# The last 64 inner rows of the experts as one K=128 product; routing constants made in the attention block; final norm in the tiles' block

## The chip, the cores and the metric

The kernel runs on one core of a Trainium2 chip. The metric is the device time of one execution in microseconds (us); three executions of the kernel before are given, and one more was profiled.

## What is computed

Two post-norm layers on x of shape (8, 512, 256), all in float32: 4,096 tokens of width 256.

```python
x = layernorm(x + attention_with_biases(x))            # 16 heads of 16, full
h = x + causal_attention(rmsnorm(x, g1))               # 16 heads of 16, with rope
y = h + moe(rmsnorm(h, g2))                            # 8 experts, top 2, inner size 704
out = layernorm(x + y)

def moe(xf):                                           # weights wg, wu (256 x 704), wd (704 x 256) per expert
    probs = softmax(xf @ w_router); topw, topi = top_k(probs, 2)
    g = silu(xf @ wg[e]); u = xf @ wu[e]
    return sum over the two experts of topw_normalised * ((g * u) @ wd[e])
```

## The kernel before, in words

Float32 products are made on TensorE (PE) as sums of float16 products: a value is split into a high part and a low part (what the rounding to float16 left), and a product is high x high + high x low + low x high, accumulated in one PSUM region.

The program is a row of stages. `attention_layers` (both attentions, the split of the experts' weights into parts, the router's logits) is one block of five engine programs; `route_tokens` (which tokens go to which expert, VectorE (DVE) mostly) is the next; `expert_tiles` follows, then `combine` (sum of the residual and the final layer norm). Each stage ends in two steps: the block's own end, at which every engine drains and meets the others (L271 for the attention, L1279 for the routing, L1484 for the tiles, L1734 for the final stage; the numbers are the lines that the profile gives), and `stage_semaphores`, which clears the stage's semaphores and has all engines meet again (L55, L56). Work of the next stage starts only after that.

**Routing.** GpSimd (POOL) writes eleven small constants (`iota`, `memset`, one `affine_select`; L1329 to L1345), counted by the semaphore `made`. DVE first clears rows 64 to 127 of the last chunk of `w_down` (L1397), then waits for `made` to reach 11 and for its own clearing, and then runs a chain of some 60 operations, each waiting for the one before. SyncE (SP) loads the weights of expert 0 meanwhile, then those of experts 1 to 3 (`load_experts`, L1263 to L1270), each expert waiting for the loads of the one before.

**Tiles.** Rows sorted by expert are worked on in 39 tiles of 256 rows. In tile after tile PE turns the gathered x (8 transposes, L1591), makes gate and up products in three groups (66 matmuls with 256 columns, L1606) and the down product of the tile before (36 matmuls, L1628), the latter between group 0 and group 1 of the following tile. The inner size 704 is 5 chunks of 128 rows and a sixth of 64 (`FT` = 6, `FR` = 64). The down product reads h (high part, low part) as the stationary operand and `w_down` as the moving one, once for each half of 128 rows:

```python
for half in range(2):
    for f in range(FT):
        for hh, wh in ((0, 0), (0, 1), (1, 0)):
            mm = pe.matmul(ps_y[:, s, half], h[:, s, hh, f, ...], w_down[:, e, wh, f, :])
```

So the sixth chunk takes three matmuls of a half like the others, with rows 64 to 127 of both operands zero. ScalarE (ACT) makes silu and the high part of h (L1669 to L1680), DVE the product gate x up (L1709) and the low part (L1715); the sixth chunk's are instructions on 64 partitions. DVE also scales the result by the token's share (L1697). POOL issues, on its own queue, the gathers of x (L1538) and of the shares (L1564) and the scatter that adds y into `h` in DRAM (L1552, two for a tile); a scatter waits until that of the tile before has landed. After the last tile POOL waits for the last two tiles' scatters and ends its program.

**Final stage** (`combine`). SP loads the eight sequences (512 KB each, L1750) from `h`; DVE takes mean and variance (L1776, L1779), POOL makes scale and shift in four small operations (L1764 to L1769), ACT applies them (32 activations, L1787), SP stores (L1753). POOL writes three constants first (L1759).

Of the kernel before, what the change touches and what calls it, by code (L numbers as in the profile page):

```python
# [214 lines left out]
def attention_layers(nc, t, xT_dram, x_dram, x1_dram, matrices):  # L215
# [55 lines left out]
    with ExitStack() as ctx:  # L271
# [57 lines left out]
        w_hi, w_lo, rest_filled = sem("w_hi"), sem("w_lo"), sem("rest_filled")  # L329
        block = ctx.enter_context(nc.Block())  # L330
# [181 lines left out]
        def _(pool):  # L512
# [109 lines left out]
            for n in range(FIRST, LAST):  # L622
                u, g = n // G, n % G
                if n % 2 == 0:
                    h = (n + 6) // 2
                    if plain(h // 2):
                        split_high(h)
                        split_low(h)
                    if g == 0:
                        factors(u - 2)  # L630
                        split_x(u + 2)
                    else:
                        part_low(u - 2)
                    turn_half(h)
                else:
                    h = (n + 5) // 2
                    if causal(h // 2):
                        split_high(h)
                        split_low(h)
                    if g == 1:  # L640
                        bias(u - 1)
                    normalise((n - 3) // 2)
                    if g == 3:
                        add_residual(u - 1)
                for m in weights_at(n):
                    split_weights(m)

# [606 lines left out]
def load_experts(sync, t, experts):  # L1254


    for e in experts:
# [6 lines left out]
        if e > 0:  # L1264
            sync.wait_ge(t.down_loaded, 64 * e)
        for hl in range(2):
# [3 lines left out]
            sync.dma_start(t.w_down[0:FR, e, hl, FT - 1], down[(FT - 1) * P:F]).then_inc(t.down_loaded, 16)  # L1270


def route_tokens(nc, t):
# [5 lines left out]
    with ExitStack() as ctx:  # L1279
# [3 lines left out]
        rank = sb("rank", [P, NT, E], F32)  # L1283
# [7 lines left out]
        earlier, ones = sb("earlier", [P, P], F32), sb("ones", [P, P], F32)  # L1291
        totals = sb("totals", [P, E, NT], F32)
        keep = sb("keep", [P, E, NT], F32)
# [7 lines left out]
        own = sb("own", [P, HI], F32)  # L1301
        tile_start = sb("tile_start", [P, MT, 1], F32)
# [3 lines left out]
        count_hi, count_lo = sb("count_hi", [P, 1, HI], BF16), sb("count_lo", [P, 1, P], BF16)  # L1306
# [4 lines left out]
        tile_no, row_no = sb("tile_no", [P, 2 * NT, 1], BF16), sb("row_no", [P, 1], F32)  # L1311
# [4 lines left out]
        made, did, exp_done, totalled, hot_done, by_row_done, inverse_mm, turned = map(sem, (  # L1316
            "made", "did", "exp_done", "totalled", "hot_done", "by_row_done", "inverse_mm", "turned"))
# [9 lines left out]
        @block.gpsimd  # L1327
        def _(pool):
            iota = lambda out, pattern, base, mult: pool.iota(  # L1329
                out, pattern, base=base, channel_multiplier=mult,  # L1330
                allow_small_or_imprecise_dtypes=True).then_inc(made, 1)
            iota(rank[:], [[0, NT], [-1, E]], E, 0)
            iota(tile_start[:], [[SLOT, MT]], 0, 0)
            iota(count_hi[:], [[1, HI]], 0, 0)
            iota(count_lo[:], [[1, P]], 0, 0)
            iota(tile_no[:], [[1, 2 * NT]], 1, 0)
            iota(row_no[:], [[0, 1]], 0, 1)
            iota(own[:].rearrange("p (m h) -> p m h", h=REST // P), [[0, MT], [P, REST // P]], P - T - REST, 1)
            pool.memset(ones[:], 1.0).then_inc(made, 1)
            pool.memset(keep[:], 1.0).then_inc(made, 1)  # L1340
            pool.wait_ge(made, 9)

            pool.affine_select(out=earlier[:], in_=ones[:], pattern=[[1, P]], compare_op=ALU.is_gt, fill=0.0,
                               base=0, channel_multiplier=-1).then_inc(made, 1)
            pool.memset(keep[:, :, 0:1], 0.0).then_inc(made, 1)  # L1345
            pool.wait_ge(made, 11)

        MADE = 11
# [19 lines left out]
        def _(pe):  # L1368
            pe.wait_ge(made, MADE)
# [17 lines left out]
        def _(vector):  # L1387
# [89 lines left out]
def expert_tiles(nc, t):  # L1477
# [6 lines left out]
    with ExitStack() as ctx:  # L1484
# [16 lines left out]
        cleared, h_cleared = sem("indices_cleared"), sem("h_cleared")  # L1501
# [4 lines left out]
        gu_mm, gate_out, h_out, h_hi, h_lo = map(pair, ("gu_mm", "gate_out", "h_out", "h_hi", "h_lo"))  # L1506
        block = ctx.enter_context(nc.Block())
# [6 lines left out]
        def _(sync):  # L1514
# [5 lines left out]
            sync.wait_ge(t.down_loaded, 64 * E)  # L1520

        @block.gpsimd
        def _(pool):

            pool.memset(take[:], 0).then_inc(cleared, 1)
# [54 lines left out]
            for s in range(2):  # L1580
                pool.wait_ge(stored[s], 32 * (LAST + 2 - s))

        @block.tensor
        def _(pe):
# [30 lines left out]
            def down(r, s):  # L1615
                e = expert_of(r, s)
                pe.wait_ge(t.down_loaded, e * 64 + 64)
                pe.wait_ge(y_out[s], r)
                for half in range(2):
                    c = 0  # L1620
                    for f in range(FT):
# [4 lines left out]
                        for hh, wh in ((0, 0), (0, 1), (1, 0)):  # L1626
# [3 lines left out]
                                           start=c == 0, stop=c == 3 * FT - 1)  # L1630
# [16 lines left out]
            pe.wait_ge(h_cleared, 1)  # L1647
# [10 lines left out]
        def _(act):  # L1658
# [29 lines left out]
            tile(LAST + 1, 0, None)  # L1688

        @block.vector  # L1690
        def _(vector):
# [8 lines left out]
            def tile(r, s, before):  # L1700
                for i in range(FG):
# [20 lines left out]
            vector.memset(h[FR:P, :, :, FT - 1], 0.0).then_inc(h_cleared, 1)  # L1722
# [7 lines left out]


def combine(nc, t, out):

    with ExitStack() as ctx:  # L1734
        sem = ctx.enter_context(stage_semaphores(nc, "c_"))
        sb = lambda n, s, d: ctx.enter_context(nc.sbuf_tensor("c_" + n, s, d))
        z, res = sb("z", [P, B, QT, D], F32), sb("res", [P, B, QT, D], F32)
        stats, mean_var = sb("stats", [P, B, QT, 6], F32), sb("mean_var", [P, B, QT, 2], F32)
        small = sb("small", [P, B, 4, QT], F32)
        constants = sb("constants", [P, 3, QT], F32)  # L1740
        loaded = [sem(f"loaded{b}") for b in range(B)]
        stored, stat_out, aggregated, power, mid_out, rstd_out, shift_out, done = map(sem, (
            "stored", "stat_out", "aggregated", "power", "mid_out", "rstd_out", "shift_out", "done"))
        block = ctx.enter_context(nc.Block())
        rows = lambda x, b: x[b * S:(b + 1) * S].rearrange("(p q) n -> p q n", q=QT)

        @block.sync
        def _(sync):
            for b in range(B):
                sync.dma_start(z[:, b], rows(t.h_dram[REST:], b)).then_inc(loaded[b], 16)  # L1750
            for b in range(B):
                sync.wait_ge(done, QT * (b + 1))
                sync.dma_start(rows(out, b), res[:, b]).then_inc(stored, 16)  # L1753
            sync.wait_ge(stored, 16 * B)

        @block.gpsimd
        def _(pool):
            for i, value in enumerate((-0.5, LN_EPS, -1.0)):
                pool.memset(constants[:, i], value).then_inc(power, 1)  # L1759
            pool.wait_ge(power, 3)  # L1760
            for b in range(B):
                pool.wait_ge(aggregated, QT * (b + 1))  # L1762
                mean, var = mean_var[:, b, :, 0], mean_var[:, b, :, 1]
                pool.tensor_tensor(small[:, b, 0], var, constants[:, 1], ALU.add).then_inc(mid_out, 1)  # L1764
                pool.tensor_tensor(small[:, b, 2], mean, constants[:, 2], ALU.mult).then_inc(mid_out, 1)  # L1765
                pool.wait_ge(mid_out, 2 * b + 2)
                pool.tensor_tensor(small[:, b, 1], small[:, b, 0], constants[:, 0], ALU.pow).then_inc(rstd_out, 1)  # L1767
                pool.wait_ge(rstd_out, b + 1)
                pool.tensor_tensor(small[:, b, 3], small[:, b, 2], small[:, b, 1], ALU.mult).then_inc(shift_out, 1)  # L1769

        @block.vector
        def _(vector):
            for b in range(B):
                vector.wait_ge(loaded[b], 16)
# [5 lines left out]

        @block.scalar
        def _(act):
            for b in range(B):
                act.wait_ge(rstd_out, b + 1)
                act.wait_ge(shift_out, b + 1)  # L1785
                for q in range(QT):
                    act.activation(res[:, b, q], z[:, b, q], ACT.Identity, bias=small[:, b, 3, q:q + 1],  # L1787
                                   scale=small[:, b, 1, q:q + 1]).then_inc(done, 1)


def feed_forward_kernel(nc, a, out):

    with ExitStack() as top:
# [13 lines left out]
        t.tile_expert = sb("tile_expert", [P, MT], I32)  # L1807
        with ExitStack() as ctx:
# [14 lines left out]
        with ExitStack() as ctx:  # L1823
# [9 lines left out]
            expert_tiles(nc, t)  # L1833
            combine(nc, t, out)
# [33 lines left out]
```

## Time and profile before

| | |
|---|---|
| time, median of 3 runs | 1481.46 us (1475.09, 1481.46, 1482.32) |
| the profiled execution | 1479.55 us |
| its span in the trace | 1477.6 us |
| PE busy | 1279.7 us, 87% of the span |
| DVE / ACT / POOL busy | 949.5 / 829.9 / 801.2 us |
| attention stage | up to about 913 us |
| routing | 915 to 957 us |
| expert tiles | 958 to 1444 us |
| final stage | 1450 to 1477.6 us |

Busy times of engines overlap. The span runs from the first to the last instruction; the profiled execution's own time is 1.95 us longer than its span. A stage's time is set by the engine or chain that ends it, which the timelines of its end show.

### The profile page before, as it was taken

How to read it: one execution, taken by the hardware profiler on the slowest of the kernel's cores; microseconds unless marked ns; L12 is line 12 of the kernel's file. 1: busy time of each engine (PE TensorE's matmuls, PEld its weight loads, DVE VectorE, ACT ScalarE, POOL GpSimd, SP SyncE). 2: the span in 40 equal slices, each digit the busy share in tenths (PEclk: the TensorE clock that was granted, in tenths of full speed). 3: DMA queues.
4: the chain of work that ended last, by engine and by line, in shares of the span. 5: the costliest groups of instructions: out<-in, count | busy, mean ns of one | idle time of the engine just before them, and what ended most of it. 6: DMA issues, size and time to landing. Idle time of an engine off the chain costs nothing. (4 is left out here: it accounts for less than half of the span.)

```text
span 1477.6 us, 33278 instructions
## 1 busy us (share of the span) xinstructions
PE 1279.7 (87%) x11533; PEld 712.1 (48%) x11534; DVE 949.5 (64%) x1766; ACT 829.9 (56%) x1672; POOL 801.2 (54%) x834
## 2 busy tenths in 40 slices
PE   1699999999999999999999963389999999999980
PEld 0222222232323444444444432378888888888870
DVE  6378888888898887977888613834444444444433
ACT  4148787888888776666676741133444344333334
POOL 2322565475546566765564333056666666666643
PEclk9769999999999999999999975589999999999995
DMA  4416767676767878887775534693222222222326
GB/s 127 86 36 171 179 180 200 188 197 201 196 178 216 216 224 210 234 217 207 166 190 156 132 95 129 178 261 61 43 43 44 45 46 43 43 43 44 42 29 235
DMA packets 158365, 204.21 MB, mean 138 GB/s; under 512 B 31088, under 2 KB 120688, under 8 KB 158256
## 3 DMA queue, kind: packets, MB, share of 16 engines
q1 hardware_dynamic: 140784, 182.29, 45.3%
q0 software_dynamic: 17472, 20.50, 8.9%
q8 instruction: 64, 1.05, 0.3%
q14 instruction: 45, 0.37, 0.1%
HBM read 111.20 MB, written 82.87 MB: 131 GB/s over the span
## 5 line engine op out<-in xcount | busy, mean ns | idle before, releaser
L987 ACT ACTIVATE a_probs<-a_ps_s 128x512 f32<-128x512 f32 (+2 forms) x896 | 460.0, 569 | 159.4 <-PE a_ps_s L782 154.3
L1056 DVE TENSOR_REDUCE a_shift_max<-a_ps_m 128x1 f16<-128x512 f32 x512 | 320.4, 682 | 70.5 <-PE a_ps_m L787 69.1
L787 PE MATMUL a_ps_m<-a_qkx 48*128 48x128 f16 (+3 forms) x1408 | 284.3, 301 | 21.1 <-DMA a_qkx<-a_qk_dram 8.9
L1606 PE MATMUL e_ps_gu<-e_xT,w_up 128*128 128x256 f16 x2574 | 297.8, 273 | 2.6 <-ACT e_xT L1661 2.4
L782 PE MATMUL a_ps_s<-a_qkx 49*128 49x128 f16 (+3 forms) x1408 | 275.4, 295 | 15.3 <-ACT a_probs L987 15.3
L1606 PEld LDWEIGHTS e_ps_gu<-e_xT,w_up 128*128 x2574 | 249.3, 98 | 36.1 <-issue 7.1
L883 PE MATMUL a_ps_o<-a_probs,a_v_one 128*32 128x512 f32 (+3 forms) x2048 | 234.1, 530 | 2.8 <-ACT a_o L994 2.7
L782 PEld LDWEIGHTS a_ps_s<-a_qkx 49*128 49x128 f16 x1408 | 89.6, 94 | 266.9 <-ACT a_probs L987 155.8
L1552 POOL DMA_INDIRECT h<-e_y,e_put x78 | 124.8, 1600 | 90.2 <-DVE e_y L1697 60.2
L1628 PE MATMUL e_ps_y<-w_down,e_h 128*128 x1404 | 162.7, 273 | 7.6 <-issue 5.0
L552 POOL TENSOR_TENSOR a_o_half<-a_o_half,a_inv_half 128x512 f32<-128x512 f32 x32 | 40.6, 1270 | 227.4 <-DMA a_inv_half<-a_inv_dram 227.4
L1709 DVE TENSOR_TENSOR e_h<-e_gate,e_ps_gu 128x512 f32<-128x512 f32 (+2 forms) x156 | 82.6, 550 | 126.2 <-ACT e_gate L1669 87.3
L1669 ACT ACTIVATE e_gate<-e_ps_gu 128x512 f32<-128x512 f32 x78 | 46.6, 597 | 200.9 <-PE e_ps_gu L1606 128.8
L1628 PEld LDWEIGHTS e_ps_y<-w_down,e_h 128*128 128x128 f16 x1404 | 127.9, 97 | 40.1 <-issue 14.9
L1056 DVE TENSOR_REDUCE a_neg_off<-a_ps_m 128x1 f32<-128x384 f32 (+2 forms) x256 | 138.1, 543 | 8.9 <-PE a_ps_m L787 8.1
L1715 DVE TENSOR_TENSOR e_h<-e_h 128x512 f16<-128x512 f32 (+2 forms) x156 | 83.5, 556 | 89.1 <-ACT e_h L1673 46.2
L539 POOL CAST a_qk<-a_q 128x1024 f16<-128x1024 f32 x32 | 33.2, 1036 | 157.6 <-DVE a_q L1111 96.0
L670 PE MATMUL a_ps_x<-a_xT,w_proj 128*128 128x512 f16 x384 | 101.6, 404 | 18.3 <-POOL a_xT L520 15.8
L787 PEld LDWEIGHTS a_ps_m<-a_qkx 48*128 48x128 f16 x1408 | 84.1, 94 | 63.9 <-DVE a_shift_max L1056 36.7
L1056 DVE TENSOR_REDUCE a_neg_max<-a_ps_m 128x4 f32<-128x512 f32 x128 | 87.7, 685 | 41.0 <-PE a_ps_m L787 40.2
L1564 POOL DMA_INDIRECT e_share<-weights,e_find x78 | 81.2, 1041 | 42.2 <-issue 42.2
L1538 POOL DMA_INDIRECT e_x<-part,e_take x78 | 81.2, 1041 | 41.5 <-issue 40.3
(195 smaller groups left out, 1661.0 us busy)
## 6 DMA issues: line engine op xcount, KB each, us to landing
a_qkx<-a_qk_dram SPq DMA_DIRECT2D x192, 128.0 KB, 4.5
a_qk_dram<-a_qk SPq DMA_DIRECT2D x32, 512.0 KB, 5.4
a_o_dram<-a_o SPq DMA_DIRECT2D x64, 256.0 KB, 2.7
a_o_half<-a_o_dram SPq DMA_DIRECT2D x32, 256.0 KB
a_inv_half<-a_inv_dram SPq DMA_DIRECT2D x32, 256.0 KB
part<-a_part SPq DMA_DIRECT2D x16, 512.0 KB, 5.8
a_q_swap<-a_q SPq DMA_DIRECT2D x64, 128.0 KB, 3.9
a_w_in<-in_wg SPq DMA_DIRECT2D x16, 352.0 KB, 5.4
```

What stands on the lines that cost most here:

```text
L670: mm = pe.matmul(ps_x[:], t.w_proj[:, 4 * layer + w, wh, k, m * P:(m + 1) * P], xT[:, u % 2, xh, k, :], start=n == 0, stop=n == 5)
L782: return pe.matmul(out, kx[first:first + 49, r, pair, kt * P:(kt + 1) * P], qx[first:first + 49, r, pair, q0:q1], start=start, stop=stop)
L787: return pe.matmul(out, qx[first:first + 48, r, pair, q * P:(q + 1) * P], kx[first:first + 48, r, pair, k0:k1], start=start, stop=stop)
L883: mm = pe.matmul(ps_o[32 * j:32 * (j + 1), S - w:S], v_one[:, u % 2, kt, g * HG + j, :], probs[:, kt // 2, j, first:first + w], start=kt = ...
L987: act.activation(dst, src, ACT.Exp).then_inc(exp_out, 1)
L1056: vector.tensor_reduce(out, src, AX.X, ALU.max, negate=True).then_inc(max_out, 1)
L1538: pool.indirect_dma_start(x[:, s, half], None, t.part_dram, bass.IndirectOffsetOnAxis(ap=take[:, s, half:half + 1], axis=0)).then_inc(gath ...
L1552: pool.indirect_dma_start(t.h_dram, bass.IndirectOffsetOnAxis(ap=put[:, s, half:half + 1], axis=0), y[:, s, half], None, compute_op=ALU.ad ...
L1606: mm = pe.matmul(ps_gu[:, bank, kind, f % 2], w[:, ds(e, 1)].rearrange("p o f -> p (o f)"), xT[:, s, xh, k, :], start=n == 0, stop=n == 5)
L1628: mm = pe.matmul(ps_y[:, s, half], h[:, s, hh, f, half * P:(half + 1) * P], w[:, ds(e, 1)].rearrange("p o f -> p (o f)"), start=c == 0, st ...
L1709: op = vector.tensor_tensor(h32[0:rows, bank, m], gate[0:rows, bank, m], ps_gu[0:rows, bank, 1, m], ALU.mult)
L1715: op = vector.tensor_tensor(h[0:rows, s, 1, f], h32[0:rows, bank, m], h[0:rows, s, 0, f], ALU.subtract)
```

## The change

Three parts.

1. The low part of h's sixth chunk (64 rows) is written into rows 64 to 127 of the high part's chunk, and rows 64 to 127 of the high `w_down` chunk hold a second copy of the same 64 weight rows. One matmul then makes high x high + low x high, a second one (with the low weights, whose rows 64 to 127 stay zero) high x low. The down product takes 34 matmuls for a tile instead of 36. Each expert's load has one more transfer (64 x 256 float16); only the low half of `w_down` is cleared, by POOL in the routing stage, and h is not cleared at all.
2. The eleven constants of the routing are written by POOL at the end of its attention program; they live in tensors of the whole kernel. The routing's DVE and PE programs no longer wait for them.
3. `combine` is gone; its instructions stand at the end of the engines' programs in the tiles' block, with the loaded sums and the results in the space of `w_up`. SP itself waits for the last scatters and then loads. POOL writes the three constants at the start of the tiles' block.

```diff
@@ attention_layers, POOL, after the loop @@
+            iota = lambda out, pattern, base, mult: pool.iota(
+                out, pattern, base=base, channel_multiplier=mult,
+                allow_small_or_imprecise_dtypes=True).then_inc(made, 1)
+            iota(t.rank[:], [[0, NT], [-1, E]], E, 0)
...
+            pool.memset(t.keep[:, :, 0:1], 0.0).then_inc(made, 1)
+            pool.wait_ge(made, 11)
@@ load_experts @@
-            sync.wait_ge(t.down_loaded, 64 * e)
+            sync.wait_ge(t.down_loaded, 80 * e)
...
-            sync.dma_start(t.w_down[0:FR, e, hl, FT - 1], down[(FT - 1) * P:F]).then_inc(t.down_loaded, 16)
+            for first in ((0, FR) if hl == 0 else (0,)):
+                sync.dma_start(t.w_down[first:first + FR, e, hl, FT - 1],
+                               down[(FT - 1) * P:F]).then_inc(t.down_loaded, 16)
@@ route_tokens @@
         def _(pool):
-            iota = lambda out, pattern, base, mult: pool.iota(
...
-            pool.wait_ge(made, 11)
+            pool.memset(t.w_down[FR:P, :, 1, FT - 1], 0.0).then_inc(padded_out, 1)
+            pool.wait_ge(padded_out, 1)
...
-            pe.wait_ge(made, MADE)
             pe.wait_ge(ready_both, 1)
...
-            vector.memset(t.w_down[FR:P, :, :, FT - 1].rearrange("p e h n -> p (e h) n"), 0.0).then_inc(padded_out, 1)
-            vector.wait_ge(made, MADE)
-            vector.wait_ge(padded_out, 1)
             source = t.logits
@@ expert_tiles @@
+        zr = w_up[:].rearrange("p e h k f -> p (e h k f)")[:, 0:4 * B * QT * D].bitcast(F32).rearrange(
+            "p (z b q n) -> p z b q n", z=2, b=B, q=QT)
+        z, res = zr[:, 0], zr[:, 1]
...
+            for s in range(2):
+                sync.wait_ge(stored[s], 32 * (LAST + 2 - s))
+            for b in range(B):
+                sync.dma_start(z[:, b], rows(t.h_dram[REST:], b)).then_inc(sum_loaded[b], 16)
...
         def _(pool):
+            for i, value in enumerate((-0.5, LN_EPS, -1.0)):
+                pool.memset(constants[:, i], value).then_inc(power, 1)
...
-                        for hh, wh in ((0, 0), (0, 1), (1, 0)):
+                        for hh, wh in ((0, 0), (0, 1)) if f == FT - 1 else ((0, 0), (0, 1), (1, 0)):
...
-                                           start=c == 0, stop=c == 3 * FT - 1)
+                                           start=c == 0, stop=c == 3 * FT - 2)
...
-            pe.wait_ge(h_cleared, 1)
             turn(0, 0)
...
-                        op = vector.tensor_tensor(h[0:rows, s, 1, f], h32[0:rows, bank, m], h[0:rows, s, 0, f],
-                                                  ALU.subtract)
+                        low = h[0:P, s, 1, f] if rows == P else h[FR:2 * FR, s, 0, f]
+                        op = vector.tensor_tensor(low, h32[0:rows, bank, m], h[0:rows, s, 0, f], ALU.subtract)
...
-            vector.memset(h[FR:P, :, :, FT - 1], 0.0).then_inc(h_cleared, 1)
             tile(0, 0, None)
```

The order of instructions moves at two places. The first is POOL at the end of the attention stage and in the routing (`L55 ISA` is the semaphore clearing between two stages, a branch the end of a block's program). Before:

```order
L608 TENSOR_TENSOR a_part<-a_hid,a_part 128x4x256
L271 UNCONDITIONAL_BRANCH
L55 ISA
L1327 UNCONDITIONAL_BRANCH
L1329 IOTA r_rank 128x256
L1329 IOTA r_tile_start 128x39
L1329 IOTA r_count_hi 128x78
```

And in the change (`a_part` is now L609; it and the first four `IOTA` stand right ahead of this piece):

```order
L649 IOTA tile_no 128x64
L649 IOTA row_no 128x1
L649 IOTA own 128x78
L659 MEMSET ones 128x128
L660 MEMSET keep 128x256
L662 AFFINE_SELECT earlier<-ones 128x128
L664 MEMSET keep 128x8
L271 UNCONDITIONAL_BRANCH
L55 ISA
L1343 UNCONDITIONAL_BRANCH
L1345 MEMSET w_down 64x8x256
```

All eleven constants now stand ahead of the block's end; between the block's end and the tiles POOL has the clearing of `w_down` alone.

The second is SP at the end of the tiles. `L1484` is the end of the tiles' block. Before:

```order
L1268 DMA w_down<-w_down_lo 128x5x256
L1270 DMA w_down<-w_down_lo 64x256
L1484 UNCONDITIONAL_BRANCH
L1747 UNCONDITIONAL_BRANCH
L1750 DMA c_z<-h 128x1024 x8
L1753 DMA out<-c_res 128x1024 x8
L1734 UNCONDITIONAL_BRANCH
```

And in the change:

```order
L1287 DMA w_down<-w_down_lo 128x5x256
L1290 DMA w_down<-w_down_lo 64x256
L1530 DMA w_up<-h 128x1024 x8
L1533 DMA out<-w_up 128x1024 x8
L1478 UNCONDITIONAL_BRANCH
```

The loads of the sums follow the weight loads in the same program, with no end of a block between.

## Rows read from the trace of the kernel before

**Rows 1.** Busy time by stretch, whole core: stretch, PE, PEld, DVE, ACT, POOL, clock, DMA, GB/s

```profile
960.00:1000.00 40.00, 33.70 (x300) 28.36 (x301) 12.30 (x23) 15.07 (x25) 22.87 (x29) 0.89 0.93 258
1100.00:1400.00 300.00, 296.21 (x2757) 253.81 (x2756) 128.71 (x251) 118.84 (x225) 198.35 (x226) 1.00 0.28 44
```

**Rows 2.** Timeline of PE, 963 to 1000 us: start, duration, instruction, idle before

```profile
979.37 4.16 PE L1628 MATMUL e_ps_y<-w_down,e_h 128*128 x36 [0.39 <-issue]
983.36 2.78 PE L1606 MATMUL e_ps_gu<-e_xT,w_up 128*128 128x256 f16 x24
...
995.23 2.78 PE L1606 MATMUL e_ps_gu<-e_xT,w_up 128*128 128x256 f16 x24
```

**Rows 3.** What PE waited for, 960 to 1440 us: us in total, times, longest

```profile
PE e_ps_xT L1591 <- DMA e_x<-part,e_take: 8.5, 1, 8.5
PE e_ps_y L1628 <- issue: 5.0, 16, 0.4
PE e_ps_y L1628 <- DVE e_h L1715: 2.6, 4, 1.6
PE e_ps_gu L1606 <- ACT e_xT L1661: 2.4, 2, 1.4
```

**Rows 4.** Timeline, 905 to 965 us, all engines

```profile
907.81 2.12 POOL L608 TENSOR_TENSOR a_part<-a_hid,a_part 128x1024 f16<-128x1024 f32 x1 [2.87 <-ACT a_part L1030]
...
912.79 0.19 DVE L1130 COPY logits<-a_ps_x 128x32 f32<-128x32 f32 x1 [0.97 <-PE a_ps_x L733]
...
914.73 0.59 POOL L1329 IOTA r_rank<- 128x256 f32 x1 [4.80 <-POOLq L56]
...
915.21 1.76 DVE L1397 MEMSET w_down<- 64x2048 uint32 x1 [2.23 <-PEq L56]
...
917.45 0.42 DVE L1402 TENSOR_REDUCE r_best<-logits 128x32 f32<-128x256 f32 x1 [0.48 <-POOL r_keep L1345]
```

**Rows 5.** Instructions of line 271, the attention block's end: duration ns, start us

```profile
L271 SPq COMPARE_BRANCH  x1: 33/33/33, 913.4 to 913.4; - x1
```

**Rows 6.** Instructions of line 1279, the routing block's end

```profile
L1279 SPq DRAIN  x1: 370/370/370, 944.1 to 944.1; - x1
L1279 DVEq DRAIN  x1: 10/10/10, 957.0 to 957.0; - x1
```

**Rows 7.** Timeline, 1435 to 1477.6 us

```profile
1440.96 1.55 POOL L1552 DMA_INDIRECT h<-e_y,e_put  x1 [0.30 <-issue]
1449.83 4.78 SPq L1750 DMA_DIRECT2D c_z<-h  x8
1449.83 0.17 POOL L1759 MEMSET c_constants<- 128x4 f32 x3 [7.32 <-POOLq L56]
...
1455.96 0.20 POOL L1764 TENSOR_TENSOR c_small<-c_mean_var,c_constants 128x4 f32<-128x4 f32 x1 [5.95 <-DVE c_mean_var L1779]
```

**Rows 8.** Instructions of line 1484, the tiles block's end

```profile
L1484 POOLq COMPARE_BRANCH  x1: 41/41/41, 1444.6 to 1444.6; - x1
L1484 POOLq DRAIN  x1: 4221/4221/4221, 1444.8 to 1444.8; - x1
```

**Rows 9.** Timeline, 1200 to 1225 us

```profile
1201.78 1.62 POOL L1552 DMA_INDIRECT h<-e_y,e_put  x1 [2.40 <-DVE e_y L1697]
...
1206.95 0.75 DVE L1715 TENSOR_TENSOR e_h<-e_h 128x256 f16<-128x256 f32 x2 [0.79 <-ACT e_h L1680]
...
1207.14 4.19 PE L1628 MATMUL e_ps_y<-w_down,e_h 128*128 x36
...
1213.11 1.62 POOL L1552 DMA_INDIRECT h<-e_y,e_put  x1 [0.86 <-POOL e_put L1546]
```

**Rows 10.** Groups by line and shape, 960 to 1440 us: ACT, then DVE

```profile
L1675 ACT ACTIVATE e_gate<-e_ps_gu 128x256 f32<-128x256 f32 x39 | 14.9, 383 | 13.6 <-PE e_ps_gu L1606 13.4 <-issue 0.2
L1676 ACT ACTIVATE e_gate<-e_ps_gu 64x256 f32<-64x256 f32 x39 | 14.8, 380 | 0.5
L1715 DVE TENSOR_TENSOR e_h<-e_h 64x256 f16<-64x256 f32 x39 | 16.0, 410 | 0.0
```

More of the change, by code:

```diff
@@ L1310, in route_tokens @@
         by_row = sb("by_row", [P, 2 * NT, HI], BF16)
-        tile_no, row_no = sb("tile_no", [P, 2 * NT, 1], BF16), sb("row_no", [P, 1], F32)
+        rank, tile_start, keep, earlier, ones = t.rank, t.tile_start, t.keep, t.earlier, t.ones
+        own, count_hi, count_lo, tile_no, row_no = t.own, t.count_hi, t.count_lo, t.tile_no, t.row_no
         inverse = sb("inverse", [P, P], F32)
@@ L1506, in expert_tiles @@
         gu_mm, gate_out, h_out, h_hi, h_lo = map(pair, ("gu_mm", "gate_out", "h_out", "h_hi", "h_lo"))
+        zr = w_up[:].rearrange("p e h k f -> p (e h k f)")[:, 0:4 * B * QT * D].bitcast(F32).rearrange(
+            "p (z b q n) -> p z b q n", z=2, b=B, q=QT)
+        z, res = zr[:, 0], zr[:, 1]
+        stats, mean_var = sb("stats", [P, B, QT, 6], F32), sb("mean_var", [P, B, QT, 2], F32)
+        small = sb("small", [P, B, 4, QT], F32)
+        constants = sb("constants", [P, 3, QT], F32)
+        sum_loaded = [sem(f"sum_loaded{b}") for b in range(B)]
+        out_stored, stat_out, aggregated, power, mid_out, rstd_out, shift_out, done = map(sem, (
+            "out_stored", "stat_out", "aggregated", "power", "mid_out", "rstd_out", "shift_out", "done"))
+        rows = lambda x, b: x[b * S:(b + 1) * S].rearrange("(p q) n -> p q n", q=QT)
         block = ctx.enter_context(nc.Block())
@@ L1519, in _ @@
                 sync.wait_ge(t.up_loaded[hl], 48 * E)
-            sync.wait_ge(t.down_loaded, 64 * E)
+            sync.wait_ge(t.down_loaded, 80 * E)
+            for s in range(2):
+                sync.wait_ge(stored[s], 32 * (LAST + 2 - s))
+            for b in range(B):
+                sync.dma_start(z[:, b], rows(t.h_dram[REST:], b)).then_inc(sum_loaded[b], 16)
+            for b in range(B):
+                sync.wait_ge(done, QT * (b + 1))
+                sync.dma_start(rows(out, b), res[:, b]).then_inc(out_stored, 16)
+            sync.wait_ge(out_stored, 16 * B)
         @block.gpsimd
         def _(pool):
+            for i, value in enumerate((-0.5, LN_EPS, -1.0)):
+                pool.memset(constants[:, i], value).then_inc(power, 1)
             pool.memset(take[:], 0).then_inc(cleared, 1)
@@ L1581, in _ @@
                 pool.wait_ge(stored[s], 32 * (LAST + 2 - s))
+            pool.wait_ge(power, 3)
+            for b in range(B):
+                pool.wait_ge(aggregated, QT * (b + 1))
+                mean, var = mean_var[:, b, :, 0], mean_var[:, b, :, 1]
+                pool.tensor_tensor(small[:, b, 0], var, constants[:, 1], ALU.add).then_inc(mid_out, 1)
+                pool.tensor_tensor(small[:, b, 2], mean, constants[:, 2], ALU.mult).then_inc(mid_out, 1)
+                pool.wait_ge(mid_out, 2 * b + 2)
+                pool.tensor_tensor(small[:, b, 1], small[:, b, 0], constants[:, 0], ALU.pow).then_inc(rstd_out, 1)
+                pool.wait_ge(rstd_out, b + 1)
+                pool.tensor_tensor(small[:, b, 3], small[:, b, 2], small[:, b, 1], ALU.mult).then_inc(shift_out, 1)
         @block.tensor
@@ L1688, in _ @@
             tile(LAST + 1, 0, None)
+            for b in range(B):
+                act.wait_ge(rstd_out, b + 1)
+                act.wait_ge(shift_out, b + 1)
+                for q in range(QT):
+                    act.activation(res[:, b, q], z[:, b, q], ACT.Identity, bias=small[:, b, 3, q:q + 1],
+                                   scale=small[:, b, 1, q:q + 1]).then_inc(done, 1)
         @block.vector
@@ L1729, in _ @@
             empty_y(LAST + 1, 0)
[L1732 to L1748, printed above, removed]
-            for b in range(B):
[L1750 to L1774, printed above, removed]
@@ L1779, in _ @@
                     vector.bn_aggr(mean_var[:, b, q], stats[:, b, q]).then_inc(aggregated, 1)
[L1781 to L1788, printed above, removed]
 def feed_forward_kernel(nc, a, out):
@@ L1807, in feed_forward_kernel @@
         t.tile_expert = sb("tile_expert", [P, MT], I32)
+        t.rank, t.tile_start = sb("rank", [P, NT, E], F32), sb("tile_start", [P, MT, 1], F32)
+        t.keep, t.earlier, t.ones = sb("keep", [P, E, NT], F32), sb("earlier", [P, P], F32), sb("ones", [P, P], F32)
+        t.own = sb("own", [P, HI], F32)
+        t.count_hi, t.count_lo = sb("count_hi", [P, 1, HI], BF16), sb("count_lo", [P, 1, P], BF16)
+        t.tile_no, t.row_no = sb("tile_no", [P, 2 * NT, 1], BF16), sb("row_no", [P, 1], F32)
         with ExitStack() as ctx:
```

48 lines of the change are left out of this document (19 added, 29 removed).

## The prediction

> **What bounds the kernel now.** I read four views in turn: busy time by stretch, what PE waits for among the tiles, the timelines of the two stage borders that the change touches, and the instructions at the ends of the blocks. The reader should see three different limits. Among the tiles PE is busy 296.21 of 300 us at the full granted clock [rows 1], and all its waits from 960 to 1440 us sum to 18.5 us, 8.5 of them one wait for the first gather [rows 3]: a matmul removed there is worth its own time. In the routing PE has nothing to do and one chain of DVE operations sets the end; it starts at 917.45 us, when POOL's last constant is there [rows 4]. In the final stage loads, DVE, POOL and ACT follow one another, and everything hangs on when the first load is issued, 1449.83 us [rows 7].
>
> **Part 1, the down product.** It removes 2 matmuls of 36 in each of 39 tiles, 78 in all. The price of one comes from start to start, since ends overlap: 36 matmuls fill 979.37 to 983.36 us, 111 ns each [rows 2]; over 300 us the mean is 296.21/2757 = 107 ns, narrower transposes included [rows 1]. I take 111: 78 x 0.111 = 8.7 us (8.4 at the least). All of it is on the path unless another engine has to be waited for, and two could be.
>
> DVE: the low part of the sixth chunk must be there when PE gets to chunk 4, where it waits for both last chunks. In the tile at 1207 us the pair of low operations ends at 1206.95 + 0.75 = 1207.70, and PE, which begins at 1207.14, is 12 matmuls or 1.33 us further at 1208.47 [rows 9]: 0.77 us of slack, and nothing ahead of chunk 4 changes. The operation itself, on 64 partitions (0.410 us) [rows 10], now writes to other partitions than it reads. No row shows DVE doing that; the nearest is ACT, which reads rows 64 to 127 and writes rows 0 to 63 in 380 ns, beside 383 ns for the same width unshifted [rows 10]. So zero; the price of its being otherwise is the last rival.
>
> POOL: from one scatter to the next it needs 1213.11 - 1201.78 = 11.3 us in a tile in which its own copy, not y, was what it waited for last [rows 9]. PE's tile takes 995.23 - 983.36 = 11.87 us [rows 2] and would take 11.65. That is 0.3 us of room, thin but enough.
>
> The extra weight transfers (one for each expert, 32 KB) go to SP's queue. For experts 0 to 3 SP is done at 944.1 us while DVE comes to the block's end at 957.0 [rows 6]; four more transfers at the 4.78/8 = 0.6 us that SP takes to issue one [rows 7] are far below 12.9. Experts 4 to 7 are loaded while the first tiles run, with the DMA engines 93% busy [rows 1], and PE did not wait for them [rows 3]. Zero, at worst 1 us where they meet the gathers. The clearing of h is hidden behind the first gather's 8.5 us [rows 3]: zero.
>
> **Part 2, the constants.** DVE's first useful operation starts at 917.45 us; without its own clearing of 1.76 us and the wait for POOL it starts where the clearing did, 915.21 [rows 4]. Gain 2.24 us, and the chain behind it moves as a whole. The constants take POOL 917.45 - 914.73 = 2.7 us at most [rows 4]. At the end of the attention POOL is free from 907.81 + 2.12 = 909.93 us [rows 4], so it would be done by 912.7, while DVE's last copy ends at 912.98 and SP comes to the block's end at 913.4 [rows 4, 5]. They are covered with 0.7 us to spare; without the cover they would cost at most their 2.7 us. The clearing of half of `w_down` on POOL has the whole DVE chain as cover. On the other side POOL now writes three more constants ahead of the first gather: 0.17 us [rows 7], exposed, since PE waits for that gather.
>
> **Part 3, the final norm.** POOL sees the last scatters landed at 1444.6 us and goes to the block's end. There its drain takes 4.221 us [rows 8], then come the meeting, the clearing and the second meeting, and SP issues the first load at 1449.83 [rows 7]. In the change SP waits for the same semaphores itself and can issue at about 1444.7: a gain of 5.1 us. What the drain waits for is not shown. POOL's last scatter instruction ended at 1442.51 [rows 7], so it is nothing that I can name. If POOL really is occupied until 1449.0 us, the norm does not suffer: its first small operation stands at 1455.96 now [rows 7] and would be due at 1455.96 - 5.1 = 1450.9. Everything behind the first load moves as it is. The Trainium skill (VectorE: DVE Perf Modes, The DRAIN you can't avoid) says that the drains around a program, on all five engines, are about 12 ns constant, beside a longer one that belongs to DVE's operations. By that rule a drain on POOL is worth nothing by itself, and the 4.2 us would be something else that stays; the row says 4.221 us, and the sum goes by the row.
>
> **Sum.** 8.7 + 2.24 + 5.1 - 0.17 = 15.9 us less. The profiled execution took 1479.55 us, so the changed kernel should take 1463.7, rounded to 1464. The median of the three runs is 1.9 us above the profiled one and the lowest 4.5 below it, so the sum may be off by that alone.
>
> **Rivals.** *The time behind the drain stays.* What occupied POOL for 4.2 us could hold the loads or POOL's small operations as well, past the point worked out above. Then only the rest of the border is saved, 5.2 - 4.2 = 1.0 us, and the time is 1463.7 + 4.1 = 1468. For it: the cause of the drain is unknown. Against: POOL already knows at 1444.6 that the data have landed. *The tile's length is not PE's.* If POOL's chain of 11.3 us with its scatters, or a wait that PE's model hides, sets the 11.87, 78 matmuls give nothing: 1463.7 + 8.7 = 1472.4. For it: the 0.3 us of room; against: PE's few waits [rows 3] and its 99% of busy time [rows 1]. *The constants are not covered.* POOL may be slower at them beside the attention's last work; past 0.7 us of slack up to 2 us come back, 1466. *Slower: PE waits for the shifted low part.* If DVE's write to other partitions takes 0.41 + t, PE waits t - 0.77 in every tile. The gains are used up at t = 0.77 + 15.9/39 = 1.18 us, that is an operation of 1.6 us, four times its present length; from 1.37 us on the kernel is slower by over 0.5%. At five times (t = 1.64) it is 34 us of waiting, 1498. For it: no DVE row with a shift. Against: ACT's pair of rows, where the shift costs nothing [rows 10].
>
> **Chances.** The forecast as it stands 0.66, the drain's time staying 0.13, no gain in the tiles 0.10, constants exposed 0.06, slower 0.05. The spread of the runs before gives the forecast's own range, 1459 to 1467; adding the case of the drain and that of the constants reaches 1471. What is left out are the two ends, together a little under 0.2 with the noise. A measurement of this kernel can tell some 0.5% (7.4 us) from no change. Faster by more than that: 0.66 + 0.13 + 0.06 and a small part of the 1472 case, 0.87; within it 0.08; slower 0.05.
>
> **What would show it.** Down matmuls 1326 instead of 1404; a tile of 11.65 us; DVE's first reduce of the routing right after the stage border, 2.2 us earlier against the end of the attention; the first load of the sums within 0.3 us of the last scatters' landing, and POOL's long drain, if it is still there, beside ACT's work. I am wrong if PE shows waits for L1715's successor or for gathers in most tiles, if POOL's constants end after SP's arrival at the attention's end, or if the first small operation of POOL in the final norm starts later than 2 us after the first load has landed.

## The result and the profile after

The changed kernel takes 1460.6 us (median of 4 runs, 1459.44 to 1469.85) against 1478.28 us before (4 runs, 1474.09 to 1482.32): a ratio of the means of 0.9892 (a fifth run of the change, 1461.24 us, is in it), 95% interval 0.9847 to 0.9938, or 16 us less; the medians lie 17.7 us apart. The forecast was 15.9 us less, 1464 us, with a range of 1459 to 1471.

The profiled execution of the changed kernel is the longest of its four, 1469.85 us with a span of 1468.1. Its attention stage, which the change hardly touches, ended 7.3 us later than in the profile of before: the last copy of the logits starts at 920.06 us instead of 912.79. Over all thirteen traces of this study that moment lies between 907.5 and 920.1 us, with and without the constants, so whole spans say little here and stages say much. What follows compares lengths inside the two traces. From the start of that copy to the end of the span it is 1477.6 - 912.79 = 564.8 us before and 1468.1 - 920.06 = 548.0 after: 16.8 us less.

Busy time by stretch of the changed kernel (columns as in rows 1):

```profile
1100.00:1400.00 300.00, 295.84 (x2757) 254.29 (x2755) 134.22 (x258) 120.45 (x229) 199.30 (x231) 1.00 0.28 45
```

PE is as busy as before and does as many matmuls in 300 us, 2757 [rows 1]; a tile merely needs 108 of them instead of 110. Its timeline, to be held against rows 2:

```profile
1195.88 3.93 PE L1654 MATMUL e_ps_y<-w_down,e_h 128*128 x34 [0.30 <-issue]
1199.64 2.78 PE L1632 MATMUL e_ps_gu<-e_xT,w_up 128*128 128x256 f16 x24
...
1207.35 3.97 PE L1654 MATMUL e_ps_y<-w_down,e_h 128*128 x34
1211.16 2.78 PE L1632 MATMUL e_ps_gu<-e_xT,w_up 128*128 128x256 f16 x24
```

Here 34 matmuls fill 3.76 us, still 111 ns each, and this tile takes 11.52 us. Tiles come in two lengths that take turns: from the start of the third down product to that of the 35th the mean of a tile is 11.99 us before (mostly 11.7 and 12.3) and 11.75 after (mostly 11.4 and 12.1). What PE waited for, 960 to 1437 us (rows 3):

```profile
PE e_ps_xT L1617 <- DMA e_x<-part,e_take: 8.5, 1, 8.5
PE e_ps_y L1654 <- issue: 5.4, 17, 0.4
PE e_ps_y L1654 <- DVE e_h L1747: 2.3, 3, 1.6
PE e_ps_gu L1632 <- ACT e_xT L1686: 1.4, 1, 1.4
```

No wait took the place of the removed work. Timeline of the border from attention to routing (rows 4):

```profile
915.09 2.12 POOL L609 TENSOR_TENSOR a_part<-a_hid,a_part 128x1024 f16<-128x1024 f32 x1 [2.87 <-ACT a_part L1049]
...
917.16 0.59 POOL L649 IOTA rank<- 128x256 f32 x1
...
919.74 0.11 POOL L664 MEMSET keep<- 128x8 f32 x1
920.06 0.19 DVE L1149 COPY logits<-a_ps_x 128x32 f32<-128x32 f32 x1 [0.96 <-PE a_ps_x L752]
922.00 1.80 POOL L1345 MEMSET w_down<- 64x2048 f16 x1 [2.15 <-POOLq L56]
...
922.04 0.42 DVE L1396 TENSOR_REDUCE r_best<-logits 128x32 f32<-128x256 f32 x1 [1.79 <-PEq L56]
```

and who came to the block's end when (rows 5):

```profile
L271 POOLq DRAIN  x1: 34/34/34, 920.0 to 920.0; - x1
L271 DVEq DRAIN  x1: 223/223/223, 920.1 to 920.1; - x1
L271 SPq COMPARE_BRANCH  x1: 38/38/38, 920.7 to 920.7; - x1
```

The constants fill the gap between POOL's last work and SP's arrival. They end at 919.85 us, some 0.85 us ahead of it, and with POOL's drain some 0.6 us. The final stage (rows 7) and the end of the tiles' block (rows 8):

```profile
1436.66 1.55 POOL L1568 DMA_INDIRECT h<-e_y,e_put  x1 [0.30 <-issue]
1440.55 3.74 SPq L1530 DMA_DIRECT2D w_up<-h  x8
...
1446.26 0.20 POOL L1602 TENSOR_TENSOR e_small<-e_mean_var,e_constants 128x4 f32<-128x4 f32 x1 [8.04 <-DVE e_mean_var L1766]
```

```profile
L1478 POOLq DRAIN  x1: 4487/4487/4487, 1459.6 to 1459.6; - x1
L1478 ACTq DRAIN  x1: 3972/3972/3972, 1460.0 to 1460.0; - x1
L1478 SPq COMPARE_BRANCH  x1: 33/33/33, 1466.5 to 1466.5; - x1
```

The first load follows the start of the last scatter instruction by 3.89 us, 8.87 before [rows 7]. POOL's drain has not gone. It is 4.487 us long, more than 20 us after the last scatter, and lies beside ACT's last work and the stores, where it costs nothing. POOL's first small operation comes 2.00 us after DVE's first of the final norm, 1.98 before.

### The profile page after: what moved, and what is told of

Its sections match the earlier page's. It is cut to its first block and busy times, and to the rows that moved or that the text cites. A ratio compares the mean times of both kernels' runs of the same rounds, so it can differ in the third digit from the quotient of the medians.

```text
span 1468.1 us, 33103 instructions
## 1 busy us (share of the span) xinstructions
PE 1280.0 (87%) x11455; PEld 707.7 (48%) x11456; DVE 950.6 (65%) x1764; ACT 830.1 (57%) x1672; POOL 796.7 (54%) x835
## 5 line engine op out<-in xcount | busy, mean ns | idle before, releaser
L1654 PE MATMUL e_ps_y<-w_down,e_h 128*128 x1326 | 154.1, 273 | 7.8 <-issue 5.4
L1747 DVE TENSOR_TENSOR e_h<-e_h 128x512 f16<-128x512 f32 (+2 forms) x156 | 87.7, 562 | 87.4 <-ACT e_h L1698 56.1
L1654 PEld LDWEIGHTS e_ps_y<-w_down,e_h 128*128 128x128 f16 x1326 | 121.2, 97 | 38.4 <-issue 17.2
L689 PE MATMUL a_ps_x<-a_xT,w_proj 128*128 128x512 f16 x384 | 105.4, 416 | 18.3 <-POOL a_xT L521 15.8
L1554 POOL DMA_INDIRECT e_x<-part,e_take x78 | 75.4, 967 | 41.4 <-issue 40.6
```

The lines of the kernel that those rows point to most:

```text
L689: mm = pe.matmul(ps_x[:], t.w_proj[:, 4 * layer + w, wh, k, m * P:(m + 1) * P], xT[:, u % 2, xh, k, :], start=n == 0, stop=n == 5)
L1654: mm = pe.matmul(ps_y[:, s, half], h[:, s, hh, f, half * P:(half + 1) * P], w[:, ds(e, 1)].rearrange("p o f -> p (o f)"), start=c == 0, st ...
L1747: op = vector.tensor_tensor(low, h32[0:rows, bank, m], h[0:rows, s, 0, f], ALU.subtract)
```

## The experiments

All are read from the same six lengths, in us. *Border*: start of the last logits copy to DVE's first reduce. *Chain*: from there to the start of the routing's last DVE operation. *Tiles*: first gate/up matmul to the end of the last down product. *Load*: start of the last scatter instruction to the first load of the sums. *Final*: from the first load to the end of the span. *Rest*: logits copy to the end of the span.

| kernel | border | chain | tiles | load | final | rest |
|---|---|---|---|---|---|---|
| before | 4.66 | 39.1 | 471.5 | 8.87 | 27.8 | 564.8 |
| the change | 1.98 | 39.0 | 462.6 | 3.89 | 27.6 | 548.0 |
| `p1_only` | 4.66 | 38.1 | 462.0 | 8.98 | 27.2 | 553.9 |
| `p2_both` | 1.97 | 39.2 | 471.1 | 8.88 | 27.3 | 561.4 |
| `p3_only` | 4.65 | 39.1 | 471.5 | 3.97 | 27.4 | 559.6 |
| `after_again` | 1.96 | 39.0 | 461.4 | 3.71 | 27.5 | 546.5 |
| `p2_consts` | 4.24 | 39.2 | 471.1 | 9.03 | 27.1 | 563.6 |
| `drain_early` | 4.67 | 39.1 | 470.2 | 6.64 | 27.3 | 560.8 |
| `drop_low` | 1.97 | 39.0 | 438.0 | 3.94 | 27.2 | 523.2 |
| `drop_most` | 1.99 | 39.0 | 436.4 | 3.93 | 27.4 | 523.6 |
| `unshifted` | 1.97 | 39.3 | 463.2 | 3.88 | 27.5 | 548.8 |
| `thirty` | 3.18 | 39.1 | 445.6 | 3.93 | 27.4 | 532.2 |
| `final_split` | 1.97 | 39.0 | 462.5 | 3.86 | 25.9 | 546.2 |

### One part at a time

The down product alone (`p1_only`), put into the kernel before:

```diff
-                        for hh, wh in ((0, 0), (0, 1), (1, 0)):
+                        for hh, wh in ((0, 0), (0, 1)) if f == FT - 1 else ((0, 0), (0, 1), (1, 0)):
...
+                        low = h[0:P, s, 1, f] if rows == P else h[FR:2 * FR, s, 0, f]
...
-            vector.memset(t.w_down[FR:P, :, :, FT - 1].rearrange("p e h n -> p (e h) n"), 0.0)
+            vector.memset(t.w_down[FR:P, :, 1, FT - 1], 0.0)
```

> The kernel before with the down product's part alone (34 matmuls of a tile; DVE clears only the low half of w_down; constants and final stage as before). Theory (each removed matmul is worth 111 ns, all on the path): from the first gate/up matmul to the end of the last down product 471.5 - 8.7 = 462.8 us, the rest unchanged; DVE's routing chain still starts when POOL's last constant is there, so the clearing that is half as long (0.9 us) gives nothing. Whole time 8.7 us less. Rival (another engine sets the tile's length): 471.5 us as before. Rival (the gain in the tiles comes from the later parts of the change, such as no barrier): 471.5.

Tiles 462.0 us, 9.5 less. Whole time: ratio 0.9936, interval 0.9914 to 0.9958, 9.5 us less (6 to 13). The part gives its gain alone. The rest is 10.9 us less, since the chain is 1.0 us and the final stage 0.6 us shorter in this one trace. Of the chain, 0.84 us is one group of 16 matmuls that DVE waits for: 1.93 us before, with a granted clock of 0.66 from 950 to 955.5 us, and 1.09 us here at 1.00. Nothing in the edit touches that group. DVE's shorter clearing gives nothing, border 4.66: POOL's constants hold it at the same moment.

The constants and the clearing (`p2_both`):

```diff
+            iota(t.rank[:], [[0, NT], [-1, E]], E, 0)          # and ten more, end of POOL's attention program
...
         def _(pool):
-            iota(rank[:], [[0, NT], [-1, E]], E, 0)
...
+            pool.memset(t.w_down[FR:P, :, :, FT - 1].rearrange("p e h n -> p (e h) n"), 0.0).then_inc(padded_out, 1)
```

> The kernel before with the constants written at the attention's end and the clearing of w_down (both halves, 64 x 4096 float16) on POOL in the routing; the final stage's sums and results lie in the space of w_up, since the constants need the room, which should change nothing. Theory: from the last copy of the logits to DVE's first reduce of the routing 4.66 us before, 1.98 us now as in the change (2.7 less); attention's end unchanged; tiles 471.5 us; whole time 2.2 to 2.7 us less. Rival (the constants push the attention's end out): SP no longer comes last at the block's end and the time to the reduce stays above 3 us.

Border 1.97 us, 2.69 less, and the rest of the lengths unchanged. In the whole time the ratio is 0.9993, interval 0.998 to 1.0006, that is 3.0 us less to 0.9 us more. The stage's 2.7 us lie just inside, and so does zero: whole times do not show this part, the border does. The rival that the constants push the attention's end out has nothing for it: that end comes at 912.6 us in the mean of the nine traces with the constants there and at 912.3 in the four without.

The final norm (`p3_only`):

```diff
+            for s in range(2):
+                sync.wait_ge(stored[s], 32 * (LAST + 2 - s))
+            for b in range(B):
+                sync.dma_start(z[:, b], rows(t.h_dram[REST:], b)).then_inc(sum_loaded[b], 16)
...
-def combine(nc, t, out):
```

> The kernel before with the final norm in the tiles' block alone. Theory: from the start of the last scatter instruction to the first load of the sums 8.87 us before, 3.9 us now, 5.0 us less in all; POOL's drain of 4.2 us still there but beside ACT's work. Rival (what the drain waits for holds the loads): 8 us from scatter to load. Whole time 5 us less, or 1 us less by the rival.

Load 3.97 us instead of 8.87: 4.9 less, and nothing held the loads. Whole time: ratio 0.9957, interval 0.9929 to 0.9985, 6.4 us less (2 to 10).

> The changed kernel once more, on the chip of the three parts. Theory: the parts add up, 8.9 + 2.7 + 5.0 - 0.1 = 16.5 us less than before in stage lengths; whole time 14 to 18 us less. Rival (the parts overlap): clearly less than the sum of the three.

Ratio 0.9868, interval 0.9837 to 0.9899: 19.5 us less (15 to 24); rest 564.8 - 546.5 = 18.3 us less. The three parts alone sum to 9.5 + 2.7 + 4.9 = 17.1 us in their own stage, which both traces of the change (16.8 and 18.3) frame; by their rests they would sum to 19.5, since the lengths that a part does not touch vary by up to 1 us from trace to trace. They are in series and add up within that.

### What the drain is

```diff
         @block.sync
+            for s in range(2):
+                sync.wait_ge(stored[s], 32 * (LAST + 2 - s))
...
         @block.gpsimd
-            for s in range(2):
-                pool.wait_ge(stored[s], 32 * (LAST + 2 - s))
```

> The kernel before, with the wait for the last scatters at the end of the tiles' block on SP and no longer on POOL, whose program ends with its last scatter instruction. Theory A (the drain is a fixed 4.2 to 4.5 us once POOL has issued transfers in that block, whenever it runs): it starts 1.6 us after the last scatter instruction starts and ends 6 us after it, while the data land 3.7 us after it; the first load of the sums comes 8.87 - 2.1 = 6.8 us after the start of the last scatter instruction. Theory B (the drain waits for something of the scatters that ends 8 us after the last one): the drain is longer, about 6.3 us, and the first load stays at 8.9 us.

Theory A. Instructions of line 1484 in this kernel, and its last scatter and first load:

```profile
L1484 POOLq DRAIN  x1: 7430/7430/7430, 1441.9 to 1441.9; - x1
L1484 SPq COMPARE_BRANCH  x1: 33/33/33, 1447.3 to 1447.3; - x1
```

```profile
1443.56 1.55 POOL L1554 DMA_INDIRECT h<-e_y,e_put  x1 [0.30 <-issue]
1450.20 3.88 SPq L1750 DMA_DIRECT2D c_z<-h  x8
```

The drain's row begins before the last scatter instruction, since POOL's queue reaches it early; it ends at 1441.9 + 7.43 = 1449.3, 4.2 us after that instruction's end at 1445.11. SP sees the data landed at 1447.3, 2 us before the drain is over. So the 4.2 us start where POOL's last work ends and do not depend on the landing. In the change the row begins under POOL's last operation, which ends at 1459.79 us, and ends 4.25 us after it. Before, they started only after the wait for the landing and were added to it. With the wait on SP the first load comes 2.2 us sooner (6.64 for 8.87); with the end of the block out of the way, 5.0. What POOL does in those 4.2 us no run tells. In blocks in which POOL had issued no transfers (attention, routing, final stage) its drain was over 0.07 to 0.22 us after its last operation. That the transfers are the cause is not shown: the tiles' block is the only one with them.

### The two halves of the wait at the routing's start

```diff
-            vector.wait_ge(made, MADE)
             vector.wait_ge(padded_out, 1)
```

> The kernel before with the constants written at the attention's end, while DVE still clears both halves of w_down at the start of the routing (sums and results in the space of w_up). Theory: the two halves of the wait at the routing's start cover each other, so moving one alone gives little: DVE's first reduce comes when its clearing of 1.76 us ends, 1.98 + 1.8 = 3.8 us after the last copy of the logits starts being followed by the border (4.66 before, 1.98 in the change). It also shows whether the clearing started 0.48 us after POOL's first constant because POOL was at work: without POOL's work it should start at once. Rival (the whole gain is POOL's constants): 2.0 us.

```profile
909.35 0.19 DVE L1149 COPY logits<-a_ps_x 128x32 f32<-128x32 f32 x1 [0.97 <-PE a_ps_x L752]
911.30 0.36 SPq L1282 DMA_DIRECT2D w_up<-w_up_hi  x1
...
911.79 1.76 DVE L1391 MEMSET w_down<- 64x2048 uint32 x1 [2.24 <-PEq L56]
...
913.59 0.42 DVE L1395 TENSOR_REDUCE r_best<-logits 128x32 f32<-128x256 f32 x1
```

Moving the constants alone gives 0.4 us; with the clearing it is 2.7. The size expected (3.8) was missed by 0.44 us: the clearing starts 0.49 us after SP's first load although POOL is idle, while the reduce in the changed kernel starts 0.04 us after it (922.00 and 922.04 above). A first instruction that is this clearing comes some 0.45 us later than one that is the reduce. In `p1_only`, whose clearing is half as long (0.91 us), it comes 0.28 us after SP's first load, so the delay shrinks with the clearing. POOL's work is not the cause; what is stays open.

### How far the tiles are PE's

`drop_low` leaves out high x low of h and weights in five chunks, `drop_most` all but high x high, `thirty` high x low in two chunks:

```diff
-  for hh, wh in ((0, 0), (0, 1)) if f == FT - 1 else ((0, 0), (0, 1), (1, 0)):
+  for hh, wh in ((0, 0), (0, 1)) if f == FT - 1 else ((0, 0), (1, 0)):        # drop_low, 24 of a tile
+  for hh, wh in ((0, 0),):                                                     # drop_most, 12 of a tile
+  for hh, wh in ... else ((0, 0), (1, 0)) if f in (1, 2) else ...:             # thirty, 30 of a tile
```

> The changed kernel without the product of h's high part with the weights' low part in the first five chunks: 24 down matmuls of a tile instead of 34. This part of the computation is left out. Theory A (PE alone sets the tile's length): 10 x 0.111 = 1.1 us less a tile, 43 us less in all, a tile of 10.4 us. Theory B (POOL's chain of about 11.0 us a tile, read from the trace of the change, is next behind PE's 11.6): a tile of about 11.0 us, 20 to 25 us less in all, POOL no longer waits for y.

> The changed kernel with only the product high x high in the down product: 12 matmuls of a tile instead of 34. The products with the low parts are left out (of h's low part only the sixth chunk's is in). Theory A (PE alone): 22 x 0.111 = 2.4 us less a tile, 95 us less in all, a tile of 9.2 us. Theory B (POOL next at about 11.0 us a tile): the same time as the kernel with 24 matmuls, within 3 us.

> The changed kernel with 30 down matmuls of a tile instead of 34 (high x low is left out for two of the six chunks). 36, 34, 24 and 12 matmuls gave tiles of 471.1, 462.0, 438.0 and 436.4 us in length. Theory (PE sets the length down to where POOL's chain of about 11.05 us a tile takes over, at some 28 to 29 matmuls): still on PE's line, 462.0 - 39 x 4 x 0.114 = 444 us, with 0.117 us for each as measured between 36 and 34, or 0.111 as read from the trace: 443.7 to 444.7. Rival (the two limits mix long before the crossing): clearly above, 448 or more.

Theory B for the first two. Tiles 438.0 and 436.4 us for 24 and 12 matmuls: twelve more taken away are worth 1.6 us in 39 tiles. Busy time by stretch, first of `drop_low`, then of `drop_most`:

```profile
1100.00:1400.00 300.00, 280.84 (x2585) 237.03 (x2583) 138.80 (x266) 127.11 (x240) 213.94 (x236) 1.00 0.29 45
```

```profile
1100.00:1400.00 300.00, 250.03 (x2180) 198.45 (x2180) 132.43 (x258) 123.84 (x231) 212.69 (x233) 0.99 0.29 45
```

PE falls from 296 us busy to 281 and 250, and POOL goes from 199 to 213 in both. What POOL waited for in the change, 1000 to 1400 us, and then in `drop_low`, 1000 to 1390:

```profile
POOL h L1568 <- DVE e_y L1728: 43.5, 28, 2.3
```

```profile
POOL h L1568 <- issue: 39.2, 69, 1.8
```

The 43.5 us that POOL waited for y are gone; before each scatter it now has only its own gaps. Its chain of copies, issues and gaps is the bound. From the third tile's scatter to the 35th's it takes 11.38 us a tile in `drop_low` and 11.43 in `drop_most`, against 11.75 in the change. That is 0.4 us a tile, or 12 of the 24 us. Another 10 us come from the last four tiles (34.6 us instead of 45.0 from the 35th scatter to the last), where POOL soon has no gathers left and does not bound. With 30 matmuls the tiles take 445.6 us, 0.9 above the 443.7 to 444.7 expected; 462.3, the mean of the five kernels with 34, less 156 x 0.111 is 445.0. PE's line holds down to there within the 1.9 us by which the five differ, and no further than about there: POOL's scatters stand 11.34 us apart in `thirty`. (Its border of 3.18 us is SP arriving 1.2 us later at the attention's end.)

### The shifted write

```diff
-                        low = h[0:P, s, 1, f] if rows == P else h[FR:2 * FR, s, 0, f]
+                        low = h[0:rows, s, 1, f]
```

> The changed kernel with the low part of h's sixth chunk written to rows 0 to 63 of the low tensor again, where no matmul reads it (h's rows 64 to 127 are cleared as before). The sixth chunk's low part of h is thus left out of the result. It tells what makes the 64-row subtraction take 421 ns in the change and with the down product's part alone, and 410 ns before and with the final norm's part alone. Theory (the write to other partitions): 410 ns here. Rival (something else of the changed down product): 421 ns. The tiles' length stays at 461 to 463 us by both, since the operation has slack.

The subtraction on 64 partitions, as groups by shape, in the change and in `unshifted` (before: 410 ns, no idle time, [rows 10]):

```profile
L1747 DVE TENSOR_TENSOR e_h<-e_h 64x256 f16<-64x256 f32 x39 | 16.4, 421 | 0.5
```

```profile
L1748 DVE TENSOR_TENSOR e_h<-e_h 64x256 f16<-64x256 f32 x39 | 16.1, 413 | 0.0
```

413 ns, nearer to 410: writing 64 partitions further makes the operation itself about 10 ns longer (medians 419 and 409). The larger cost is in its start. The pair of subtractions, in the change:

```profile
1207.21 0.86 DVE L1747 TENSOR_TENSOR e_h<-e_h 128x256 f16<-128x256 f32 x2 [0.79 <-ACT e_h L1705]
```

Before and in `unshifted` the pair takes 0.75 us [rows 9]. Its members, 425 and 410 ns, overlap there by 83 ns. In every trace with the shifted write the second starts 14 ns after the first has ended, in all 39 tiles, which is the 0.5 us of idle time in the row. The shifted write thus costs 0.11 us a tile. It does not matter to PE: the pair ends at 1208.07 us in the tile shown, PE, which begins at 1207.35, gets there at 1208.68, and the tiles take 463.2 us unshifted against 461.4 to 462.6 in the four other kernels with 34 matmuls.

### A little more of the final stage

```diff
-                for q in range(QT):
+                for q in range(QT - b % 2):
                     act.activation(res[:, b, q], z[:, b, q], ACT.Identity, ...
...
+                for c in [b - 2] * (b >= 3 and b % 2) + [b] * (b == B - 1):
+                    vector.tensor_scalar(res[:, c, QT - 1], z[:, c, QT - 1], small[:, c, 1, QT - 1:QT],
+                                         small[:, c, 3, QT - 1:QT], ALU.mult, ALU.add).then_inc(done_v, 1)
```

> The changed kernel with 4 of ACT's 32 operations of the final norm given to DVE (the last quarter of sequences 1, 3, 5 and 7, each two sequences later in DVE's order, the last one at the end). Theory (ACT's row of 0.49 us operations sets the end after the first load): 4 x 0.49 = 2.0 us less from the first load to the end, 25.5 instead of 27.5 us. Rival (DVE, which gets 4 x 0.5 us more on top of 13.5 us, or the stores set it now): 26.5 us or more. In the whole time 1 to 2 us, which three rounds cannot tell from none.

Final 25.9 us, 1.6 less than the 27.5 of `after_again` (27.2 to 27.6 in the seven traces with the final norm in the tiles' block and ACT doing all of it); the theory of ACT's row holds, at four fifths of its size. In the whole time it takes 1463.94 us (ratio to before 0.9896, 0.9873 to 0.9918), which cannot be told from the change's 0.9892 and 0.9868. It is not shown to beat it.

## Why the prediction was right

**Part 1**, 8.7 us expected. The kernels that have 36 matmuls average 471.1 us in the tiles (five traces), those with 34 average 462.3 (five traces): 8.7 us, 112 ns for each of the 78. In the one pair of profiles it was 8.9. Price and argument held, and so did the two zeros in what they cost PE. In the prediction DVE's shifted write was put at nothing by the likeness of an ACT operation, and that reading was wrong: it costs DVE 0.11 us a tile, which the 0.77 us of slack covers. POOL had room. The room was read as 0.3 us from one tile of each engine, and the means over 32 tiles put it at 11.75 - 11.38 = 0.4. That two single tiles gave nearly the right room is luck in part: PE's tiles take turns between two lengths, and the 11.87 us that was read is neither. The trace of before could not show POOL's own chain well, because in about half of its tiles (17 waits from 1000 to 1400 us) POOL waited for y.

**Part 2**, 2.24 us expected, 2.69 found (border 4.66 to 1.97). The cover of the constants held, with some 0.85 us to spare where 0.7 was read. The sum was short by 0.45 us since it took DVE's first operation to start where the clearing had started. The three constants ahead of the first gather cost 0.1 us (last DVE operation of the routing to the first clearing of `take`: 1.22 to 1.32), not 0.17.

**Part 3**, 5.1 us expected, 5.0 found. The step on the drain was right in its result, and the rival that its time stays was wrong in place: it does stay, as a row of 4.487 us, but on POOL alone, where nobody needs POOL. "It is nothing that I can name" remains half true: a fixed 4.2 us after POOL's last work or wait in the block with transfers of its own, cause unknown. The rule of the Trainium skill (VectorE: DVE Perf Modes, The DRAIN you can't avoid) that the prediction weighed, about 12 ns for the drains around a program on all engines, does not cover this one: the row says 4.221 us, and that decides.

**Sum.** 15.9 us expected; 16.8 and 18.3 in the two traces' rests, 16.0 (9 to 23) and 19.5 (15 to 24) in the two sets of timed runs. The base was the weaker number: 1464 was reckoned from a profiled 1479.55 us where the median of before is now 1478.28 over four runs and 1478.44 over fourteen; the medians of the change are 1460.6 and 1460.4. The timed runs alone could not have told the three terms apart; the stage lengths do.

## What to carry to other kernels

A stage border is priced by each engine's own arrival and drain, not by a flat figure: here one engine's drain was 4.2 of 5.2 us, and it was paid in series only because that engine also had to wait for the data; moving the wait to an engine with a cheap drain hid 2.2 us of it, and moving the border away as well gave 5.0. Where two preparations cover each other, moving one gives little and moving both gives much more: 0.4 us for the constants alone, nothing for halving the clearing, 2.7 for both. When the busiest engine loses work, test how far its line goes by taking away far more than is planned: here the next bound, POOL's issuing, stands only 0.4 us a tile behind, three or four matmuls.

## What the runs showed of the hardware

- A drain on POOL ended 4.22 to 4.25 us after POOL's last operation or wait at the end of the one block in which POOL had issued indirect transfers, whether these had just landed, had landed 20 us before, or were still on their way when the 4.2 us began; 0.07 to 0.22 us after the last operation in blocks without them (attention, routing, final stage).
- DVE's write shifted by 64 partitions, 64 x 256, behind an unshifted one: it starts 14 ns after that one's end instead of 83 ns before it and takes 421 ns in the mean against 410 to 413, together 0.11 us.
- The attention stage of near-identical programs ended between 907.5 and 920.1 us. In the two profiles set side by side first, TensorE's granted clock from 500 to 650 us was 0.95 after and 0.98 before:

```profile
500.00:650.00 150.00, 139.57 (x1538) 61.74 (x1540) 116.16 (x214) 100.65 (x216) 98.14 (x87) 0.95 0.78 215
```

```profile
500.00:650.00 150.00, 140.55 (x1574) 62.72 (x1571) 121.58 (x213) 102.62 (x222) 98.89 (x89) 0.98 0.81 221
```

PE gets through 36 matmuls fewer after than before in the same time. Over the thirteen traces the clock of this stretch and the attention's end go together: 907.5 and 907.7 us in the two with 1.00, 915.9 and 920.1 in the two with 0.95. Which of the two causes the other, or what causes both, no run tells. The 7.3 us between the two profiles is larger than two of this change's three parts, so those were read from stages.
